# An LSTM with a second recurrent layer on one core: x\*Wx0 with seven block products for eight, the second layer in 256-column matmuls, and sums moved to GpSimd

## What is computed

```
xW = einsum('ntd,dk->tnk', x, Wx0) + b0          # k = 4*512
a = xW[t] + h @ Wh0                              # LSTM step
i, f, o = sigmoid(a[:, :H]), sigmoid(a[:, H:2H]), sigmoid(a[:, 2H:3H]);  g = tanh(a[:, 3H:])
c = f*c + i*g;   h = o*tanh(c)
y0[:, t] = x[:, t] + h
h1 = tanh(y0[:, t] @ Wx1 + b1 + h1 @ Wh1)        # second layer
y[:, t] = y0[:, t] + h1
```

## Time and profile before

| | before |
|---|---|
| median of 3 runs | 2287.63 us |
| the profiled execution: time, span | 2287.48 us, 2285.6 us |
| TensorE busy | 2242.9 us (98%), 65564 records |
| TensorE weight loads | 1617.4 us (71%) |
| VectorE busy | 1974.7 us (86%) |
| ScalarE busy | 1642.1 us (72%) |
| GpSimd busy | 1.8 us, 10 instructions |
| granted TensorE clock, mean | 0.998 of full speed |

### The profile page before, as it was taken

How to read it: one execution, slowest core, us unless ns; L and a number is a source line. 1 busy time by engine, 2 the same in 40 slices (tenths; PEclk the granted TensorE clock), 3 DMA queues, 4 the chain that set the end, 5 groups by cost and what they waited for, 6 DMA issues and landing times.

```text
span 2285.6 us, 150617 instructions
## 1 busy us (share of the span) xinstructions
PE 2242.9 (98%) x65564; PEld 1617.4 (71%) x65564; DVE 1974.7 (86%) x10283; ACT 1642.1 (72%) x5662; POOL 1.8 (0%) x10
## 2 busy tenths in 40 slices
PE   5999999999999999999999999999999999999997
PEld 2677777777777777777777777777777777777775
DVE  6888888888888888888888888888888888888887
ACT  5777777777777777777777777777777777777775
POOL 0000000000000000000000000000000000000000
PEclk9999999999999999999999999999999999999999
DMA  5000000000000000000000000000000000000000
GB/s 209 9 23 18 23 18 23 13 18 23 23 18 20 16 18 23 22 19 13 18 23 23 18 23 13 18 23 23 18 13 18 23 23 18 23 14 18 23 13 13
DMA packets 16738, 54.03 MB, mean 24 GB/s; under 512 B 2256, under 2 KB 2384, under 8 KB 14800
## 3 DMA queue, kind: packets, MB, share of 16 engines
q1 hardware_dynamic: 16080, 44.41, 5.5%
HBM read 27.62 MB, written 16.78 MB: 19 GB/s over the span
## 4 chain that ended last, share of the span: by engine, by line
PE 97%; DVE 2%; ACT 1%; issue 1%; POOL 0%; DVEq 0%; ACTq 0%; POOLq 0%
PE rec_ps L178 39%; PE in_ps L178 38%; PE rnn_ps L178 20%; ACT wh_part L478 1%; DVE largest_slice L277 0%; DVE turned L353 0%; DVE wh_part L321 0%; DVE uv L365 0%; DVE h_parts L381 0%; DVE pre_sb L359 0%; ACT gates_cell L502 0%; DVE h_parts L389 0%; ACT wx_sb L466 0%; DVE turned L403 0%; ACT rnn_ps L498 0%
## 5 line engine op out<-in xcount | busy, mean ns | idle before, releaser
L178 PE MATMUL in_ps<-wx_sb,x_sb 128*32 128x512 f32 x8192 | 977.4, 594 | 22.4 <-ACT wx_sb L466 22.4
L178 PE MATMUL rec_ps<-wh_part,h_parts 128*32 128x256 f16 x32704 | 988.9, 273 | 4.4 <-DVE h_parts L389 4.4
L178 PEld LDWEIGHTS rec_ps<-wh_part,h_parts 128*32 128x32 f16 x32704 | 867.5, 97 | 12.1 <-issue 7.0
L353 DVE STREAM_TRANSPOSE turned<-rec_ps 128x256 f32<-128x256 f32 x1024 | 460.4, 450 | 201.2 <-PE rec_ps L178 155.7
L178 PEld LDWEIGHTS in_ps<-wx_sb,x_sb 128*32 128x32 f32 x8192 | 258.9, 110 | 332.1 <-issue 318.9
L178 PEld LDWEIGHTS rnn_ps<-wx_sb,y 128*32 128x32 f32 x8192 | 247.0, 110 | 302.6 <-issue 301.1
L488 ACT ACTIVATE rec_ps<-in_ps,mask_scaled 128x256 f32<-128x256 f32 x1022 | 405.8, 434 | 2.0 <-PE in_ps L178 1.6
L178 PE MATMUL rnn_ps<-wh_part,h_parts 128*32 128x128 f16 x16352 | 323.4, 219 | 7.9 <-DVE h_parts L417 7.9
L178 PE MATMUL rnn_ps<-wx_sb,y 128*32 128x128 f32 x8192 | 318.4, 273 | 1.3 <-ACT rnn_ps L498 1.3
L502 ACT ACTIVATE gates_cell<-gate_ps,unscale 128x128 f32<-128x128 f32 x511 | 187.5, 367 | 181.2 <-DVE gate_ps L359 181.2
L498 ACT ACTIVATE rnn_ps<-rnn_ps,mask_scaled 128x128 f32<-128x128 f32 x511 | 174.8, 342 | 188.4 <-DVE turned L403 188.1
(11 more groups left out here) (52 smaller groups left out, 1272.9 us busy)
## 6 DMA issues: line engine op xcount, KB each, us to landing
x_sb<-xT SPq DMA_DIRECT2D x32, 512.0 KB, 3.7
yT<-y SPq DMA_DIRECT2D x64, 256.0 KB, 2.0
wh_sb<-wh SPq DMA_DIRECT2D x5, 1024.0 KB, 9.6
wx_sb<-wx SPq DMA_DIRECT2D x5, 1024.0 KB, 18.1
b_sb<-b SPq DMA_DIRECT2D x1, 256.0 KB, 2.7
b_sb<-b SPq DMA_DIRECT2D x1, 64.0 KB, 12.2
h_first<-h0T SPq DMA_DIRECT2D x1, 32.0 KB, 19.9
```

Source lines behind the costliest of these rows:

```text
L178: last = nc.tensor.matmul(out[QUAD * q:QUAD * (q + 1)], states, weights(q), start=False, stop=True, tile_position=(0, QUAD * q), skip_grou ...
L353: nc.vector.transpose(turned0[:, half].rearrange("p b n -> p (b n)"), rec0_ps[t % 2][half][:, 0:COLSH]).then_inc(turned0_done[half], 1)
```

## The change

**x\*Wx0.** The unit is now a span of four steps (two pairs, A1 and A2), split once more in k and in columns into blocks of 2 x 2. Eight block products of 256 columns become seven, by sums and differences of the x blocks (`sum_x`, four per chunk of 16 steps, each 2 x 4 x 32 = 256 elements wide) and of the weight blocks (`sum_wx0`, four, each 2 x 4 x 256 = 2048 wide, once), both on GpSimd. A span is 14 units (7 products x 2 k) of 4 matmuls of 256 fp32 columns; they run in four slots of 4, 3, 4 and 3 units, five steps ahead at the most. Between the products the accumulators are passed on by copies: begin_c11 and copy_v on ScalarE, begin_c12 and finish_c22 (256 wide, from PSUM plus SBUF) on VectorE; `bias_z` and `bias_v` take bias0's place. `first_span` does the first four steps with eight products. `input1` takes three of its four k in the even step and one in the odd.

**LSTM's PSUM.** Half 1 has one bank instead of two (`rec0_second_ps`); its seed is issued at the start of its own step, and there are semaphores for each half.

**Second layer.** `recurrent1` streams the high and the low part of Wh1 as one matmul of 256 columns: 16 matmuls for 32. seed1 writes both with half the value, turn1 transposes 256 columns, and the four partial sums are added by GpSimd (`sum1`, two instructions) instead of add1 on VectorE.

**Sums on GpSimd.** add_y0 (two instructions, the first unscales h0_full) and add_y1 move there from VectorE. On VectorE the order at the end of the step becomes gate_products(1), state_high(0), cell(1), h0_full(0), state_low(0), state_high(1), h0_full(1), state_low(1), turn1; and in two steps of four begin_c12 or finish_c22 stands at the step's head. New waits: ScalarE's h1_full on y1_done, VectorE's h0_full on h0_unscaled, VectorE's turn1 on pre1_done.

The diff, cut to its core:

```diff
...
+            def sum_x(v, i):
+                x = x_sb[:, v % 2].rearrange("p k (g r t) n -> p r k g (t n)", g=PER_CHUNK, r=2)
+                a11, a12, a21, a22 = x[:, 0, 0:SUBH], x[:, 0, SUBH:SUB], x[:, 1, 0:SUBH], x[:, 1, SUBH:SUB]
+                sums = x_sums[:, v % 2]
...
+                if i in (1, 3):
+                    pool.wait_ge(x_summed, 4 * v + i)
+                out, one, op, other = ((sums[:, 0], a21, ALU.add, a22), (sums[:, 1], sums[:, 0], ALU.subtract, a11),
+                                       (sums[:, 2], a11, ALU.subtract, a21), (sums[:, 3], a12, ALU.subtract, sums[:, 1]))[i]
+                nc.gpsimd.tensor_tensor(out, one, other, op).then_inc(x_summed, 1)
...
+                one, other = ((b12, b11), (b22, wx0_sums[:, 0]), (b22, b12), (b21, wx0_sums[:, 1]))[i]
+                nc.gpsimd.tensor_tensor(wx0_sums[:, i], one, other, ALU.subtract).then_inc(wx0_summed, 1)
...
+            reduce_largest(0)
+            for i in range(4):
+                sum_wx0(i)
...
+            def add_y0(t):
...
+                for half in range(HALVES):
+                    pool.wait_ge(h0_full_done[half], t + 1)
+                if t:
+                    pool.wait_ge(y0_done, t)
+                nc.gpsimd.tensor_scalar(h0_true[:, :], h0_full[:, :], 1.0 / H_SCALE, None, ALU.mult).then_inc(h0_unscaled, 1)
+                pool.wait_ge(h0_unscaled, t + 1)
+                nc.gpsimd.tensor_tensor(y0[:, t // PAIR % Y0_PAIRS, :, t % PAIR], slices(h0_true[:, :]),
+                                        x_sb[:, v % 2, :, t % CHUNK], ALU.add).then_inc(y0_done, 1)
+            def sum1(s):
+                pool.wait_ge(turned1_done, s + 1)
+                if s:
+                    pool.wait_ge(h1_full_done, s)
+                nc.gpsimd.tensor_tensor(half1[:, :, :], turned1[:, :, 0:2], turned1[:, :, 2:4], ALU.add).then_inc(half1_done, 1)
+                pool.wait_ge(half1_done, s + 1)
+                nc.gpsimd.tensor_tensor(slices(pre1[:, :]), half1[:, :, 0], half1[:, :, 1], ALU.add).then_inc(pre1_done, 1)
...
+            def add_y1(s):
...
+                pool.wait_ge(h1_full_done, s + 1)
+                nc.gpsimd.tensor_tensor(y1[:, slot, :, s % GROUP], y0[:, s // PAIR % Y0_PAIRS, :, s % PAIR],
+                                        slices(h1_full[:, :]), ALU.add).then_inc(y1_done, 1)
+            for t in range(END):
+                s = t - LAG
+                if 1 <= s:
+                    add_y1(s - 1)
+                if 0 <= s < STEPS:
+                    sum1(s)
+                if t < STEPS:
+                    add_y0(t)
+                if t == 1:
+                    reduce_largest(1)
+                v, c = divmod(t, CHUNK)
+                if 3 <= c < 7 and v + 1 < CHUNKS:
+                    sum_x(v + 1, c - 3)
...
+                for k_half in range(HALVES):
+                    for n, (out, second, half) in enumerate(((c11_ps, 0, 0), (c12_ps, 0, 1), (z_ps[0], 1, 0), (v_ps[0], 1, 1))):
+                        for k in range(SUBH):
...
+                            tiles(out, x_pair(0, second, k_half * SUBH + k),
+                                  lambda q: wx0_block(k_half, half)(k, q))
+            def units(g, first, end):
+                z = z_ps[g % 2]
+                products = (
+                    (z, lambda k: x_pair(g, 0, k), wx0_block(0, 0)),
+                    (v_ps[g % 2], lambda k: x_sum(g, 0, k), wx0_sum(0)),
+                    (z, lambda k: x_sum(g, 1, k), wx0_sum(1)),
+                    (c11_ps, lambda k: x_pair(g, 0, SUBH + k), wx0_block(1, 0)),
+                    (z, lambda k: x_sum(g, 2, k), wx0_sum(2)),
+                    (c12_ps, lambda k: x_sum(g, 3, k), wx0_block(1, 1)),
+                    (z, lambda k: x_pair(g, 1, SUBH + k), wx0_sum(3)),
+                )
+                sum_of = {1: 0, 2: 1, 4: 2, 5: 3}
+                for u in range(first, end):
+                    j, k = divmod(u, 2)
+                    if k == 0:
+                        if j == 0 and g % PER_CHUNK == 0:
+                            pe.wait_ge(x_in[g // PER_CHUNK % 2], loads(g // PER_CHUNK))
+                        if j in sum_of:
+                            sums_ready(g, sum_of[j])
+                    out, states, weights = products[j]
+                    last = tiles(out, states(k), lambda q: weights(k, q))
+                last.then_inc(slot_done, 1)
 
             def recurrent0(t, states, weights):
 
-                pe.wait_ge(seed0_done, t + 1)
                 for half in range(HALVES):
+                    pe.wait_ge(seed0_done[half], t + 1)
                     cols = slice(half * COLSH, (half + 1) * COLSH)
                     for k in range(SUB):
                         if t and half == 0 and k % SUBH == 0:
                             pe.wait_ge(h0_ready[k // SUBH], t)
...
-                for k in range(half * SUBH, (half + 1) * SUBH):
+                for k in (range(SUB - 1, SUB) if half else range(SUB - 1)):
...
-            def recurrent1(s, states, weights):
+            def recurrent1(s):
 
                 if s:
                     pe.wait_ge(h1_ready, s)
                 for k in range(SUB):
-                    for part in weights:
-                        last = tiles(rec1_ps, states[:, k], lambda q: part[:, k, q])
+                    if s:
+                        last = tiles(rec1_ps, h1_parts[:, k], lambda q: wh1_parts[:, k, q].rearrange("p b w c -> p (b w c)"))
+                    else:
+                        last = tiles(rec1_by_part[:, :, 0], h_first[:, k], lambda q: wh1_sb[:, k, q])
                 last.then_inc(rec1_done, 1)
...
-            for half in range(HALVES):
-                input0(0, half)
+            first_span()
+            units(1, 0, 2)
...
+                    pe.wait_ge(seed0_done[0], 2)
+                    pe.wait_ge(c11_begun, 1)
+                    units(1, 2, UNITS_OF_PART[2])
...
-                    p, half = divmod(t + 3, PAIR)
-                    if p < PAIRS:
-                        input0(p, half)
+                    if t < SLOTS:
+                        g, part = divmod(t + 5, SPAN)
+                        pe.wait_ge(seed0_done[0], t + 2)
+                        if part == 0:
+                            pe.wait_ge(z_biased, g - 1)
+                        elif part == 1:
+                            pe.wait_ge(c11_begun, g)
+                        elif part == 2:
+                            pe.wait_ge(c12_begun, g)
+                        else:
+                            pe.wait_ge(c22_done, g)
+                            if g + 1 < SPANS:
+                                pe.wait_ge(v_biased, g)
+                        units(g, UNITS_OF_PART[part], UNITS_OF_PART[part + 1])
...
+            def begin_c12(g, t):
+                dve.wait_ge(slot_done, slots_until(t - 1))
+                dve.wait_ge(v_copied, g)
+                dve.wait_ge(seed0_done[1], t + 1)
+                nc.vector.tensor_tensor(c12_ps, z_ps[g % 2], v_sb[:, :], ALU.add).then_inc(c12_begun, 1)
+            def finish_c22(g, t):
+                dve.wait_ge(slot_done, slots_until(t - 1))
+                if g >= 2:
+                    dve.wait_ge(seed0_done[1], SPAN * (g - 1))
+                nc.vector.tensor_tensor(c22_sb[g % 2][:, :], z_ps[g % 2], v_sb[:, :], ALU.add).then_inc(c22_done, 1)
...
+            def state_full(half, n):
+                cols, subs = state_cols(half)
+                if n > 1:
+                    dve.wait_ge(h0_unscaled, n - 1)
                 nc.vector.tensor_tensor(h0_full[:, cols], o_scaled[:, half], tanh_c[half],
                                         ALU.mult).then_inc(h0_full_done[half], 1)
...
                 dve.wait_ge(rec1_done, s + 1)
...
-                                        ALU.add).then_inc(pre1_done, 1)
+                if s:
+                    dve.wait_ge(pre1_done, s)
+                nc.vector.transpose(turned1[:, :].rearrange("p b r n -> p (b r n)"), rec1_ps).then_inc(turned1_done, 1)
...
+                    g, part = divmod(t + 5, SPAN)
+                    if t < SLOTS:
+                        if part == 2:
+                            begin_c12(g, t)
+                        elif part == 3:
+                            finish_c22(g, t)
                     turn0(0, t)
                     add0(0, n)
                     turn0(1, t)
@@ -444,20 +614,15 @@
                     state1_low(s - 1)
                 if lstm:
                     gate_products(1, n)
+                    state_high(0, n)
                     cell(1, n)
-                    state_high(0, n)
-                if rnn_state:
-                    add_y1(s - 1)
-                if lstm:
+                    state_full(0, n)
                     state_low(0, n)
                     state_high(1, n)
+                    state_full(1, n)
                     state_low(1, n)
                 if rnn:
                     turn1(s)
-                if lstm:
-                    add_y0(t)
```

(51 more changed lines are left out.)

164 lines of the change are left out of this document (107 added, 57 removed).

## The result

The changed kernel takes 2425.93 us (2422.04 to 2428.57), against 2288.89 for the kernel before: a ratio of 1.060 [1.058, 1.062]. It was forecast at 2243 us, and the range ended at 2330. The profiled execution has a span of 2424.3 us, 138.7 more than the span before.

The account below looks back on a forecast made before the run. The prediction took TensorE to bound the kernel at 4.35 us a step, with the step's chain just behind at 4.25. From 2287.48 us, -51 for the steps, +3 for startup and +3.5 for the end gave 2243; range 2190 to 2330.

Parts of the forecast that it names:

- -51 for the steps: Sum's main term: 510 steps at a period of 4.25 us after the change, against 4.35 before.
- the chain's floor: Recurrence's chain through the engines after the change: 4.18 us a step, 0.07 shorter than 4.25, above TensorE's 4.12.
- GpSimd beside VectorE: Two-operand VectorE instructions held by GpSimd's sums inside the steps: 0 to 0.19 us a step, 0.07 taken.
- The period before and the two floors: Steps of the kernel before: TensorE's work 4.35 us, the chain 4.25; after the change 4.12 and 4.18.
- Rival 2: GpSimd and VectorE exclude each other in the steps: period 4.37 us, 2304 us in all; chance 0.15.
- the sign that I had named for it: Sign of the forecast's disturbance between GpSimd and VectorE: steps are longer where GpSimd has sum_x.
- The prices of GpSimd: Durations of GpSimd's sums: 0.42 us 128 wide, 0.26 64 wide, 0.74 256 wide, 5.2 2048 wide.
- three-pass bound: Upper price of a GpSimd sum: two reads and one write in turn, each at 0.83 ns an element, from memsets.
- TensorE's saving: TensorE's step work falls from 4.35 to 4.12 us: 0.215 from seven products, 0.015 from the second layer.
- rival 3: pre1's two GpSimd sums hold the LSTM: at 0.70 us each the period is 4.48, 2361 us; chance 0.20.
- Startup: Before the steps: GpSimd's weight sums and the longer first span make TensorE's first step later, 3 us, 0 to 12.
- End: Some five last steps of the second layer alone, each with a longer transpose and two GpSimd sums: 3.5 us, 2 to 6.

Follow-up runs that it names:

- b1: The kernel before with one of the two k of each half of input0 left out from pair 1 on: 2246.6 us, 0.982.
- v1: e6 with x's sums on VectorE in four of 16 steps, cell(1) before state_high(0), and add_y1 behind turn1: 2265.6 us, 0.990.
- e4: The changed kernel with add_y0 and add_y1 back on VectorE; pre1's and x's sums stay on GpSimd: 2270.5 us, 0.992.
- v3: e6 with add_y1 moved from ahead of state_low(0) to behind turn1: 2279.4 us, 0.996.
- v4: v3 with another order of TensorE's recurrent matmuls, h0_full(0) ahead of cell(1), and x's sums on GpSimd in halves: 2320.0 us, 1.014.
- e1: The changed kernel without GpSimd's sums of x from the third chunk on: 2360.1 us, 1.031.
- e7: The changed kernel with add_y1 alone moved back to VectorE, between h0_full(0) and state_low(0): 2351.1 us, 1.027.
- v2: v1 with pre1's two sums on VectorE too, so GpSimd does nothing inside the steps: 2333.5 us, 1.020.
- e2: The changed kernel with a GpSimd memset of about the same length in place of x's sums from the third chunk on: 2390.3 us, 1.045.
- e5: e2 with the state's first copy on VectorE made a two-operand instruction that adds a tile of zeros: 2355.2 us, 1.029.
- e6: e4 with the weight sums on VectorE and GpSimd's first maximum ahead of the first sums of x: 2261.0 us, 0.988.

## Why the prediction was wrong, by its steps

The forecast was 183 us too low. Its sum had -51 for the steps, +3 and +3.5; measured were +115.6, +16.4 and +6.7: 167, 13 and 3 of the 183. Against my own periods the 167 are 54 for the chain's floor and 117 for GpSimd beside VectorE, less 4 because before has 4.358 and not 4.35.

**The period before and the two floors: right, and one short.** TensorE's 4.35 and the chain's 4.25 behind it hold (b1). The floor after the change was the first step that failed. I put it at 4.18: with add_y1 gone and state_high(0) ahead of cell(1), state_low(0) was to start at 3.81 instead of 3.92, and state_high(1) at 3.97 instead of 4.04. Neither came. An ordinary step of v1, where add_y1 stands behind turn1 (the step began at 1264.73):

```profile
1268.42 0.18 DVE L536 TENSOR_TENSOR h_full<-o_scaled,gate_ps 128x32 f32<-128x32 f32 x1
...
1268.64 0.19 DVE L543 TENSOR_TENSOR h_parts<-h_full,h_parts 128x32 f16<-128x32 f32 x1
```

state_low(0) starts at 3.91. It reads h0_full(0), whose instruction starts at 3.69 and takes 0.18, in the kernel before as in v1; add_y1 had run inside that time, so that taking it away gives 0.02 us. TensorE starts 0.15 us after state_low(0) ends: 3.91 + 0.19 + 0.15 = 4.25. The medians over the steps are the same in e4, v1, v3 and b1 within 0.02 us. state_high(1) starts at 4.04 in v1, 0.10 after the second tanh, as it did before (I had left 0.04 for that), and at 4.14 in e4 and 4.15 in v3, where cell(1) comes 0.10 later for the sake of state_high(0). I moved state_high(0) ahead of cell(1), but what state_low(0) waits for, h0_full(0), stayed behind cell(1). v4 has it ahead, in one of its steps of 4.16 us (it began at 944.67):

```profile
948.27 0.18 DVE L542 TENSOR_TENSOR h_full<-o_scaled,gate_ps 128x32 f32<-128x32 f32 x1
...
948.49 0.19 DVE L549 TENSOR_TENSOR h_parts<-h_full,h_parts 128x32 f16<-128x32 f32 x1
...
948.83 0.62 PE L246 MATMUL rec_first_ps<-wh_part,h_parts 128*32 128x256 f16 x16
```

h0_full(0) starts at 3.60, state_low(0) at 3.82 and TensorE at 4.16, the floor that I had in mind. In v4 TensorE also wants half 1 later; no run has one of the two without the other, so whether half 1 would have allowed 4.16 in the old order is not shown. No variant of the changed kernel has a mean under 4.286. Taking the steps of e4 (2185.8 us) against 510 x 4.18 = 2131.8, 54 us of the error are here: 36 are the median step of 4.25, and 18 are longer steps, whose cause is not known except for the 7 named with e4.

**GpSimd beside VectorE: the right mechanism with a wrong size, and it decided the case.** This term was 0.07 us a step, with 0.19 as the upper bound. From the changed kernel to e4 the steps lose 152.6 us, 0.30 a step, where the sum had 36 us. (e4 has the y sums on VectorE, so this counts their price there as nothing.) So the bound itself was too low, by three parts.
- x's sums: 0.45 us for one step in four was bounded, and half of it taken. It is 0.54 (e1): the add is held until 0.15 us after GpSimd's operation, and add_y1 behind x_sums then holds the cell's first product (0.34 us instead of 0.22). 65 us measured, about 26 in the sum.
- add_y1 was thought to graze state1_high. It meets pre_sb in each step, 0.18 us (e7). I had GpSimd's queue end 2.5 us into the step. It ends at 2.83 (1207.43 - 1204.60), since pre1 is ready at 1.71 and not 1.5, and h_true takes 0.465 us for my 0.26: a tensor_scalar of 64 elements costs as much as an add of 128.
- Who is held was counted for add0(1) and state1_high alone. What matters is that the steps of the queue follow one another: h_true and y0 do no harm by themselves, but they push add_y1 and x_sums from a harmless place to the worst (e4 against e7: 81 us for moving y0's two operations, 69 of it in the steps with x's sums).

Rival 2 named this mechanism and gave it 0.15 with 2304 us, on the same bound. That the steps with x's sums are longer, and by about the sum's length, was the sign that I had named for it.

**The prices of GpSimd: right but for one.** 457, 321, 774 and 4800 ns were measured for 0.42, 0.26, 0.74 and 5.2 us. The three-pass bound from memset rows was a good price. The Trainium skill's 4497 ns for 2048 fp32 elements (GPSIMD Engine Reference, Performance versus the Vector engine) agrees within 7%.

**TensorE's saving: right.** A record of 256 columns costs 54 ns, as said:

```profile
1202.00 1.04 PE L284 MATMUL in_ps<-wx_sums,x_sums 128*32 128x256 f32 x16
...
1202.86 0.61 PE L284 MATMUL c_ps<-wx_sb,x_sb 128*32 128x256 f32 x8
```

16 records in 0.86 us. The 0.23 us are there, and no variant had more than 0.07 of it in the mean step: e4's is 4.286. The 4.16 of v4's shortest steps is 0.19 of it.

**pre1's sums (rival 3): cleared.** ScalarE waits 0.43 us a step for pre in 510 steps, as its tanh comes later, but this delays nothing that the period waits for: e4 keeps these sums on GpSimd and runs at 4.25, and taking them away costs 68 us (v2). (That rival's own sum, 2287.48 + 510 x 0.13 + 6.5, gives 2360 us, not 2361.)

**Startup: 3 us taken, 16.4 measured, range 0 to 12.** The step followed only the weight sums' own end; they ended at 54.9 for my 48, the first having begun at 35.47. It left out that VectorE has work with two SBUF operands at that time, eight low parts that step 1 waits for, and that they would be held: 22.55 us. The same rule as in the steps, forgotten for the largest operations. Also left out was that the maximum, for which VectorE waits, was put behind other work on GpSimd.

**End: 3.5 taken, 6.7 measured, range 2 to 6.** The last steps of the second layer stand 3.49 us apart for 2.33:

```profile
2415.02 1.04 PE L284 MATMUL rnn_ps<-wh_parts,h_parts 128*32 128x256 f16 x16 [2.44 <-DVE h_parts L589]
...
2418.51 1.05 PE L284 MATMUL rnn_ps<-wh_parts,h_parts 128*32 128x256 f16 x16 [2.44 <-DVE h_parts L589]
```

My 0.68 for the transpose and the two sums gives 3.01. Most of the rest is TensorE's clock: the 16 matmuls take 1.05 us, and 0.62 in the steps. The windows view of this stretch (busy us by engine, granted clock, DMA) has the clock at 0.50, 1.2 GHz, with TensorE busy a third of the time:

```profile
2410.00:2416.00 6.00, 2.03 (x32) 1.06 (x32) 1.29 (x5) 1.28 (x4) 1.87 (x6) 0.50 0.00 0
```

In the kernel before, the steps of the earlier trace rows still had 0.63 and 0.66 us for theirs. In e4 one of these steps began with the matmuls at 0.62 us and was 3.06 us long (2257.18 to 2260.24), the next had 1.04 and was 3.48: my 3.01 was nearly right for the full clock.

## What to carry to other kernels

Before work is moved to GpSimd, write down where on VectorE's queue each of its instructions will stand, and look at the VectorE instructions with two SBUF operands: one that is on the chain and starts just behind a GpSimd operation is late by all of that operation. Work that GpSimd does beside PSUM transposes cost nothing here (pre1's sums were worth 68 us), and the order of its queue matters more than its total: two operations put ahead cost 81 us. Before an instruction is taken out from in front of another, look when the other's operand is ready: add_y1 ran while state_low(0) had to wait for h0_full(0) anyway, and taking it away gave 0.02 us.

## What the runs showed of the hardware that I had not expected

- A VectorE tensor_scalar with one SBUF operand (fp32 to fp16, 0.15 us alone) is held by a GpSimd memset, 0.89 us, where a two-operand instruction in its place was not, 0.25 us (e2, e5). Fewer operands are not safer.
- A held VectorE instruction ends up to 0.15 us after the GpSimd operation; a GpSimd operation that finds the port taken costs 0.83 us for 0.73.
- Which of two comes first is decided by 0.04 us, and it is worth 0.44 to 0.47 us in the step (e4, v3).
- GpSimd's maximum over partitions stood behind 9.50 us in which GpSimd waited for nothing that the profile shows; in e6 the sums of x behind it have 10.44 us of the same, and those behind the second maximum 7.16. A change between these kinds of GpSimd work seems to cost 7 to 10 us; no run tells what it consists of.
